# The output projection's weights in small pieces beside the token groups, their sums made by VectorE

## The reference

```python
x = x + 0.5 * ffn(layernorm(x), A, B, Wr)
x = x + attn(layernorm(x), wq, wkv, wo)
x = x + 0.5 * ffn(layernorm(x), A, B, Wr)
# in attn: attn is [tokens, 32 * 128], wo is [4096, 512]
attn = jnp.einsum('bhqk,bkhd->bqhd', probs, v).reshape(B, S, H * DV)
return jnp.einsum('bse,ed->bsd', attn, wo)
```

## Time and profile before

| | us |
|---|---|
| median of 3 runs | 1104.97 |
| lowest, highest | 1104.9, 1106.04 |
| the profiled execution | 1104.14 |
| its span, first to last instruction | 1102.3 |
| TensorE busy in the span | 1045.1 (95%) |
| VectorE, ScalarE, GpSimd busy | 697.0, 554.5, 563.5 |

### The profile page before, as it was taken

One profiled execution on the slowest core, in us unless ns is written; L12 is line 12 of the kernel. 1 busy time (PEld: TensorE's weight loads), 2 busy tenths in 40 slices (PEclk: granted clock), 3 DMA queues, 4 the chain that ended last, 5 costly groups with the idle time before them and its releaser, 6 DMA issues.

```text
span 1102.3 us, 18719 instructions
## 1 busy us (share of the span) xinstructions
PE 1045.1 (95%) x5588; PEld 899.3 (82%) x5588; DVE 697.0 (63%) x1803; ACT 554.5 (50%) x1480; POOL 563.5 (51%) x484
## 2 busy tenths in 40 slices
PE   8999999999999999999999999999677997799998
PEld 7999788888788888888888888888555876579997
DVE  6778734243476767676767776767569765565552
ACT  4112454544466666767666667676462544341110
POOL 5332288993667778877777788773055000000000
PEclk9999999999999999999999999999987998899999
DMA  9600255755334444444444444443942576540000
GB/s 370 274 0 1 109 197 219 258 210 186 102 115 134 151 154 139 147 135 150 126 135 148 152 139 147 143 158 108 393 170 95 174 272 249 228 137 10 19 19 29
DMA packets 77942, 168.16 MB, mean 153 GB/s; under 512 B 7888, under 2 KB 24272, under 8 KB 75856
## 3 DMA queue, kind: packets, MB, share of 16 engines
q1 hardware_dynamic: 77904, 167.67, 43.3%
HBM read 102.37 MB, written 63.44 MB: 150 GB/s over the span
## 4 chain that ended last, share of the span: by engine, by line
PE 85%; DMA 6%; DVE 5%; ACT 1%; POOL 1%; SPq 1%; issue 1%; DVEq 0%; ACTq 0%; POOLq 0%
PE bank L270 25%; PE bank L272 25%; PE bank L271 24%; DMA o_raw<-keep_o 5%; PE bank L530 4%; PE bank L548 2%; PE bank L519 2%; DVE o_lo L921 2%; PE bank L326 1%; DMA x<-x_in 1%; ACT o_hi L596 1%; POOL downT_lo L1614 1%; DVE ow_lo L921 1%; DVE wo_raw L1189 1%; PE bank L278 1%
## 5 line engine op out<-in xcount | busy, mean ns | idle before, releaser
L1242 POOL TENSOR_SCALAR ve<-mv 128x1 f32<-128x1 f32 x24 | 5.5, 230 | 294.1 <-DVE mv L928 293.8
L270 PE MATMUL bank<-o_lo,ow_hi 128*128 128x512 f32 x224 | 94.4, 421 | 39.4 <-DVE o_lo L921 35.8
L921 DVE TENSOR_TENSOR o_lo<-o_raw,o_hi 128x1024 fp32r<-128x1024 f32 x56 | 77.8, 1390 | 70.4 <-ACT o_hi L596 70.2
L596 ACT CAST o_hi<-o_raw 128x1024 fp32r<-128x1024 f32 x56 | 58.8, 1053 | 110.2 <-DMA o_raw<-keep_o 96.5
L642 ACT ACTIVATE bank<-bank,nmax 128x128 f32<-128x128 f32 (+1 forms) x256 | 105.7, 455 | 3.1 <-DVE nmax L1042 3.0
L1055 DVE TENSOR_SCALAR prob<-bank,rinv 128x128 f32<-128x128 f32 (+1 forms) x256 | 95.1, 413 | 4.6
L270 PE MATMUL bank<-xc_lo,wq_hi 128*128 128x512 f32 x224 | 93.6, 418 | 2.3 <-DVE qT_lo L921 1.2
L1042 DVE CUSTOM_DVE_ANT_0 bank<-bank,mask 128x128 f32<-128x128 f32 (+1 forms) x256 | 83.7, 389 | 19.1 <-PE bank L272 19.1
L272 PE MATMUL bank<-o_hi,ow_hi 128*128 128x512 f32 x224 | 92.0, 411 | 0.0
L271 PE MATMUL bank<-o_hi,ow_lo 128*128 128x512 f32 x224 | 92.0, 411 | 0.0
L270 PE MATMUL bank<-xc_lo,wk_hi 128*128 128x512 f32 x224 | 87.7, 391 | 1.8 <-DVE s7k L1083 1.5
(11 more groups left out here) (163 smaller groups left out, 3187.9 us busy)
## 6 DMA issues: line engine op xcount, KB each, us to landing
o_raw<-keep_o SPq DMA_DIRECT2D x49, 512.0 KB, 3.6
keep_v<-out_hl SPq DMA_DIRECT2D x64, 256.0 KB, 2.3
v<-keep_v SPq DMA_DIRECT2D x64, 256.0 KB, 3.6
keep_o<-att_comb SPq DMA_DIRECT2D x60, 256.0 KB, 2.5
keep_o<-att SPq DMA_DIRECT2D x45, 256.0 KB, 3.0
stage_v<-wv SPq DMA_DIRECT2D x4, 2048.0 KB, 9.2
stage_wq<-wqk SPq DMA_DIRECT2D x16, 512.0 KB, 3.3
keep_vraw<-out_raw SPq DMA_DIRECT2D x64, 128.0 KB, 2.1
```

The lines of the kernel that those rows point to most:

```text
L270: nc.tensor.matmul(dst, a_hi, b_lo, start=first, stop=False, skip_group_check=onto)
L596: return nc.scalar.copy(dst, src)
L921: return nc.vector.tensor_tensor(dst, src, hi.bitcast(F32), ALU.subtract)
```

## The change

- SyncE: the four transfers of 2 MB become 16 pieces of 512 KB, one behind the load of each group 1 to 16 (the table `WO_LOADS`; a11's two first blocks are now loaded a second time, into `wo_raw`, since s3 needs them). They share four semaphores, so that a piece waits for the landing of the fourth piece before it. The reloads become 16 pieces of the up weights (272 KB) behind groups 20 to 27 and 32 to 39, and 16 of the down weights (256 KB) behind groups 40 to 55.
- GpSimd makes no sums of weights any more.
- VectorE makes s3 ahead of groups 13, 15, 17, 20, s2 ahead of 14, 16, 18, 21 (as a22 - s3), s1 ahead of 25, 27, 29, 31 and s4 ahead of 33, 35, 37, 39. s3 now has the buffer that s1 had, and s1 lies in the place of a21.
- TensorE's six sets of transposes, VectorE's additions and the first layer norm of the next layer stand one group later where they moved.

```diff
+WO_LOADS = {1: ("a11", 2), 2: ("a11", 3), 3: ("a11", 0), 4: ("a11", 1), 5: ("a12", 0), 6: ("a12", 1), 7: ("a21", 0),
+            8: ("a22", 0), 9: ("a12", 2), 10: ("a21", 1), 11: ("a22", 1), 12: ("a12", 3), 13: ("a21", 2),
+            14: ("a22", 2), 15: ("a21", 3), 16: ("a22", 3)}
...
+        def wait_piece(eng, name, h):
+            n = PIECES.index((name, h))
+            eng.wait_ge(s[f"wo_piece{n % 4}"], 16 * (n // 4 + 1))
...
+        def dve_o_s3(dve, h):
+            for a in ("a11", "a21"):
+                wait_piece(dve, a, h)
+            if h == 0:
+                dve.wait_ge(s["scores_ready"], 8 * PAIRS)
+            nc.vector.tensor_tensor(wo_rows("s3", h), wo_rows("a11", h), wo_rows("a21", h), ALU.subtract).then_inc(s["wo_s3_s"], 1)
 
         def dve_o_s2(dve, h):
             dve.wait_ge(s["wo_s3_s"], h + 1)
-            nc.vector.tensor_tensor(wo_rows(S2, h), wo_rows(S1, h), wo_rows(A11, h), ALU.subtract).then_inc(s["wo_s2_s"], 1)
+            wait_piece(dve, "a22", h)
+            nc.vector.tensor_tensor(wo_rows("s2", h), wo_rows("a22", h), wo_rows("s3", h), ALU.subtract).then_inc(s["wo_s2_s"], 1)
...
         def dve_output(dve):
             for m in range(7, OGROUPS):
-                if m in (9, 11, 13, 15):
-                    dve_o_s2(dve, (m - 9) // 2)
+                if m in (13, 15, 17, 20):
+                    dve_o_s3(dve, (13, 15, 17, 20).index(m))
+                elif m in (14, 16, 18, 21):
+                    dve_o_s2(dve, (14, 16, 18, 21).index(m))
                 elif m in (25, 27, 29, 31):
-                    dve_o_s4(dve, (m - 25) // 2)
+                    dve_o_s1(dve, (m - 25) // 2)
+                elif m in (33, 35, 37, 39):
+                    dve_o_s4(dve, (m - 33) // 2)
                 elif m in (19, 43, 51):
                     dve_o_sum(dve, {19: 0, 43: 1, 51: 2}[m])
-                elif m in (22, 24, 46, 48):
-                    dve_back(dve, {22: 0, 24: 1, 46: 2, 48: 3}[m])
-                elif m == 52:
+                elif m in (23, 24, 47, 48):
+                    dve_back(dve, {23: 0, 24: 1, 47: 2, 48: 3}[m])
+                elif m == 53:
                     dve_back(dve, 4)
...
-        def pool_wo_sums(pool):
...
-            for h in range(4):
-                nc.gpsimd.tensor_tensor(wo_rows(S1, h), wo_rows(A21, h), wo_rows(A22, h), ALU.add).then_inc(s["wo_s1_s"], 1)
-                pool.wait_ge(s["wo_s1_s"], h + 1)
-                nc.gpsimd.tensor_tensor(wo_rows(S3, h), wo_rows(A11, h), wo_rows(A21, h), ALU.subtract).then_inc(s["wo_s3_s"], 1)
...
+        def load_wo(sp_, name, h):
+            n = ("a11", "a21", "a12", "a22").index(name)
+            i = PIECES.index((name, h))
+            if i >= 4:
+                sp_.wait_ge(s[f"wo_piece{i % 4}"], 16 * (i // 4))
+            sp_.dma_start(wo_raw[:, n, 4 * h:4 * h + 4, :].rearrange("p c n -> p (c n)"),
+                          wo[n][:, h * 8 * P:(h + 1) * 8 * P]).then_inc(s[f"wo_piece{i % 4}"], 16)
...
+        def load_beside(sp_, m):
+            if m in WO_LOADS:
+                load_wo(sp_, *WO_LOADS[m])
+            if 20 <= m < 28:
+                k, a = divmod(m - 20, 2)
+                load_again(sp_, upT_lo[:, k, :], keep_up[1][:, k * UPW:(k + 1) * UPW], "upagain_loaded", a)
+            elif 32 <= m < 40:
+                if m == 32:
+                    sp_.wait_ge(s["wo_split"], 16)
+                k, a = divmod(m - 32, 2)
+                load_again(sp_, upT_hi[:, k, :], keep_up[0][:, k * UPW:(k + 1) * UPW], "upagain_loaded", a)
+            elif m >= 40:
+                if m == 40:
+                    sp_.wait_ge(s["wo_s4_s"], 4)
+                    sp_.wait_ge(s["wo_split"], 20)
+                i, k = divmod(m - 40, 8)
+                load_again(sp_, (downT2_hi, downT2_lo)[i][:, k, :], keep_down[i][:, k * D:(k + 1) * D], "downagain_loaded")
...
-            load_tokens(sync, 1)
-            load_wo(sync, 0, "wo_a11")
-            load_tokens(sync, 2)
-            load_tokens(sync, 3)
+            for m in range(1, 4):
+                load_tokens(sync, m)
+                load_beside(sync, m)
             load_pair(sync, LAST, final=True)
-            load_wo(sync, 1, "wo_a21")
-            load_wo(sync, 3, "wo_a22")
-            for m in range(4, 7):
+            for m in range(4, OGROUPS):
                 load_tokens(sync, m)
-            load_wo(sync, 2, "wo_a12")
-            for m in range(7, OGROUPS):
-                load_tokens(sync, m)
-                if m == 4 * OG:
-                    sync.wait_ge(s["wo_split"], 16)
-                    sync.wait_ge(s["wo_s4_s"], 4)
-                    for i, t in enumerate((downT2_hi, downT2_lo)):
-                        sync.dma_start(t[:, :, :].rearrange("p k n -> p (k n)").bitcast(F32), keep_down[i]).then_inc(s["downagain_loaded"], 16)
-                elif m == 5 * OG:
-                    sync.wait_ge(s["wo_split"], 20)
-                    for i, t in enumerate((upT_hi, upT_lo)):
-                        sync.dma_start(t[:, :, :].rearrange("p k n -> p (k n)").bitcast(F32), keep_up[i]).then_inc(s["upagain_loaded"], 16)
+                load_beside(sync, m)
...
-            pool_wo_sums(pool)
...
-                if m in (18, 20, 42, 44, 49, 51):
-                    pe_back(pe, {18: 0, 20: 1, 42: 2, 44: 3, 49: 4, 51: 5}[m])
-                elif m == 54:
+                if m in (19, 21, 43, 45, 50, 52):
+                    pe_back(pe, {19: 0, 21: 1, 43: 2, 45: 3, 50: 4, 52: 5}[m])
+                elif m == 55:
                     pe_ffn_transpose(pe, NT)
```

More of the change, by code:

```diff
@@ L58 @@
 SLOTS = 3
-O_WEIGHT = (A11, A12, S2, S3, S1, A22, S4)
 O_TOKEN = (B11, B21, T2, T3, T1, N4, B22)
@@ L68 @@
 LAST = PAIRS - 1
+WO_LOADS = {1: ("a11", 2), 2: ("a11", 3), 3: ("a11", 0), 4: ("a11", 1), 5: ("a12", 0), 6: ("a12", 1), 7: ("a21", 0),
+            8: ("a22", 0), 9: ("a12", 2), 10: ("a21", 1), 11: ("a22", 1), 12: ("a12", 3), 13: ("a21", 2),
+            14: ("a22", 2), 15: ("a21", 3), 16: ("a22", 3)}
+PIECES = tuple(WO_LOADS.values())
 EPS = 1e-5
@@ L187, in build_macaron @@
         wo_raw = place("wo_raw", [P, 4, PAIRS, 2 * P], F32, at=where["xc_hi"])
-        wo_s1 = place("wo_s1", [P, PAIRS, 2 * P], F32, at=where["upT_hi"])
-        WO = {A11: wo_raw[:, 0, :, :], A21: wo_raw[:, 1, :, :], A12: wo_raw[:, 2, :, :], A22: wo_raw[:, 3, :, :],
-              S1: wo_s1[:, :, :], S2: wo_raw[:, 0, :, :], S4: wo_raw[:, 2, :, :]}
+        wo_s3 = place("wo_s3", [P, PAIRS, 2 * P], F32, at=where["upT_hi"])
+        WO = {"a11": wo_raw[:, 0, :, :], "a21": wo_raw[:, 1, :, :], "a12": wo_raw[:, 2, :, :], "a22": wo_raw[:, 3, :, :],
+              "s1": wo_raw[:, 1, :, :], "s2": wo_raw[:, 0, :, :], "s3": wo_s3[:, :, :], "s4": wo_raw[:, 2, :, :]}
+        O_OPERAND = ("a11", "a12", "s2", "s3", "s1", "a22", "s4")
         slot = 2 * 2 * P * 16
@@ L863, in o_weight_src, with wo_rows @@
             if k < 2:
-                return ow_raw[k][:, :, :]
-            return (WO[O_WEIGHT[i]] if O_WEIGHT[i] != S3 else wo_raw[:, 1, :, :])[:, 4 * h:4 * h + 4, :]
+                return ow_raw[k][:, :, :].rearrange("p c n -> p (c n)")
+            return wo_rows(O_OPERAND[i], h)
+        def wait_piece(eng, name, h):
+            n = PIECES.index((name, h))
+            eng.wait_ge(s[f"wo_piece{n % 4}"], 16 * (n // 4 + 1))
+        def wo_rows(op, h):
+            return WO[op][:, 4 * h:4 * h + 4, :].rearrange("p c n -> p (c n)")
         def act_o_weight(act, k):
@@ L1181, in dve_o_tokens, with dve_o_s1 @@
                o_hi[n][:, :, :].rearrange("p c n -> p (c n)")).then_inc(s["o_split"], 1)
-        def wo_rows(op, h):
-            t = wo_raw[:, 1, :, :] if op in (A21, S3) else WO[op]
-            return t[:, 4 * h:4 * h + 4, :].rearrange("p c n -> p (c n)")
+        def dve_o_s3(dve, h):
[4 more added lines that the diff above has]
+            nc.vector.tensor_tensor(wo_rows("s3", h), wo_rows("a11", h), wo_rows("a21", h), ALU.subtract).then_inc(s["wo_s3_s"], 1)
         def dve_o_s2(dve, h):
             dve.wait_ge(s["wo_s3_s"], h + 1)
-            nc.vector.tensor_tensor(wo_rows(S2, h), wo_rows(S1, h), wo_rows(A11, h), ALU.subtract).then_inc(s["wo_s2_s"], 1)
+            wait_piece(dve, "a22", h)
+            nc.vector.tensor_tensor(wo_rows("s2", h), wo_rows("a22", h), wo_rows("s3", h), ALU.subtract).then_inc(s["wo_s2_s"], 1)
+        def dve_o_s1(dve, h):
+            nc.vector.tensor_tensor(wo_rows("s1", h), wo_rows("a21", h), wo_rows("a22", h), ALU.add).then_inc(s["wo_s1_s"], 1)
         def dve_o_s4(dve, h):
             dve.wait_ge(s["wo_s2_s"], h + 1)
-            nc.vector.tensor_tensor(wo_rows(S4, h), wo_rows(A12, h), wo_rows(S2, h), ALU.subtract).then_inc(s["wo_s4_s"], 1)
+            nc.vector.tensor_tensor(wo_rows("s4", h), wo_rows("a12", h), wo_rows("s2", h), ALU.subtract).then_inc(s["wo_s4_s"], 1)
         def dve_o_sum(dve, block):
@@ L1452, in load_wo_first, with load_again @@
```

(9 more changed lines are left out.)

34 lines of the change are left out of this document (11 added, 23 removed).

## The result

The changed kernel takes 1061.34 us (median of 4 runs, 1060.21 to 1061.63) where the one before takes 1104.93 beside it (1104.35 to 1106.04): a ratio of 0.960, 95% interval 0.959 to 0.962. That is 43.6 us less; the forecast was 47.0 less, 1058.0, and its range 1053 to 1066. The time lies just above the narrower 1055 to 1061 that had the chance of 0.60. The profiled execution took 1061.25 us, its span 1059.5 against 1102.3.

A forecast was written before the change was run, and what follows sets the result against it. TensorE was taken as the engine to beat, held up in the output projection by late token loads and VectorE slowed beside GpSimd. Terms summed to 47.0 us: span 1102.3 to 1055.3, plus 2.7 gives 1058.0; range 1053 to 1066.

The forecast's parts named there:

- Part 1: Last head pair: output weights in 512 KB pieces remove the 8.18 stall and half clock; 11.3 us gained, bounds 8.0 to 12.
- Part 2: Groups 7 to 10: GpSimd's eight sums go to VectorE; 15.6 us gained, plus 1.7 from half clock after 843.96.
- the wait at group 21: TensorE's transposes ahead of group 21 wait 2.4 us for VectorE's addition, 1.8 longer than before; bounds 0.6 and 4.
- Part 3: FFN weight reloads in pieces: stalls of 8.28 and 7.24 and the half clock after them go; 19.5 us gained.
- Part 4: Moved transposes: the 1.7 us wait for csum goes; the second addition's 0.75 stays.
- Part 5: DMA in groups 7 to 16: a group with one piece needs 2.8 to 3.2 us; cost 1.0, bounds 0 and 3.
- What would show it: Signs in the next trace: token loads, TensorE waits, clock 1.00, VectorE near 1.2, group 7 near 806, FFN near 948.
- A: Rival: DMA bounds groups 7 to 17 at 3.2 to 3.5 us each; 5 to 10 us less gain; chance 0.12.
- B: Rival: full VectorE in groups 13 to 22, or the last pair, holds; 3.5 to 7 us less gain; chance 0.12.
- C: Rival: transfers of one group don't overlap, 4.5 us more in each of 42 groups, 1247 us; chance 0.04.
- D: Rival: pieces pile up behind SyncE's waits and come in a burst, one stall of 8; 1068 to 1075; chance 0.03.
- E: Better case: no wait at group 21 and none of DMA's, 3 to 4 us more gain, 1054 to 1055; chance 0.08.

The follow-up runs named there:

- the experiment: Changed kernel with a11, a21, a22 and a12 again loaded as whole 2 MB transfers at the old places; 1068.41 us.
- the two controls: The changed kernel run again unaltered, in the first and third batches of follow-up runs; 1062.81 us and 1061.87 us.
- the control: The changed kernel run again unaltered, in the first batch (also called the first control); 1062.81 us, ratio 0.962.
- the paired pieces: Changed kernel with the reloads' 32 pieces in pairs behind groups 20 to 23, 32 to 35 and 40 to 47; 1061.95 us.
- the later transposes: Changed kernel with the second and fourth transposes ahead of groups 22 and 46, last addition ahead of 49; 1056.79 us.
- the earlier sums and the earlier cast: Changed kernel with later transposes, s3 and s2 up to two groups earlier, group 7 cast before the last attention copy; 1054.47 us.

## Why the prediction was right, point by point

**Part 1, 11.3.** The stretch gained 9.3 in the traces, 9.2 in the experiment. The stall of 8.18 and its low clock went, though group 4's load, issued at 780.96, took until 789.1 to land and not until 785: TensorE comes to its group later still, at 795.17. Two things took back 2.2. The first group's 12 matmuls took 2.85 us before and 4.33 after (776.39 to 780.72), since the clock fell behind the same wait of 3.68; this is no part of the change (below). And a wait of 0.72 ahead of group 6 is new. VectorE's o_lo for it takes twice its time while GpSimd adds up the attention's output beside it. VectorE's timeline, then GpSimd's:

```profile
801.05 2.31 DVE L925 TENSOR_TENSOR o_lo<-o_raw,o_hi 128x1024 fp32r<-128x1024 f32 x1
```
```profile
799.91 2.37 POOL L1274 TENSOR_TENSOR att_comb<-att_comb,att 128x512 f32<-128x512 f32 x1
```

Before, the stall of group 4 and the half clock behind it had held TensorE up: that o_lo ended at 809.7, ahead of TensorE, which came to group 6 at 811.6. The sentence on "the next late one" named the softmax chain instead.

**Part 2, 15.6 + 1.7, and the wait at group 21.** From group 7 on VectorE's subtractions take 1.22 each and never more than 1.46, where one took 3.36; groups 7 to 10 take 11.0 us instead of 26.5. GpSimd's sums alone, even spread over the pieces' arrivals, cost 10.8. The full stretch from group 13 to 22 and its bill ahead of group 21 came as described: 1.93 where 2.4 was forecast, and one instruction behind another on VectorE when it comes to the addition for which TensorE waits:

```profile
847.87 1.23 DVE L925 TENSOR_TENSOR ow_lo<-wo_raw,ow_hi 128x1024 fp32r<-128x1024 f32 x1
849.01 1.22 DVE L925 TENSOR_TENSOR o_lo<-o_raw,o_hi 128x1024 fp32r<-128x1024 f32 x1
850.15 0.68 DVE L1222 TENSOR_TENSOR x<-bank,x 128x512 f32<-128x512 f32 x1
```

**Part 3, 19.5.** Measured alone: 19.75.

**Part 4, 1.7 gained, 0.75 to stay.** The wait for csum is gone. The second addition's wait did not stay at 0.75 but grew to 1.68: this term was too small by 0.9 (in the two controls the wait was 1.63 and 1.22). The reload's pieces run beside that stretch, and I gave them no price there ("Later groups ... fit"); that they are the cause, no run shows.

**Part 5, 1.0 for DMA.** A group with its piece needs 2.9 us by the trace, inside the 2.8 to 3.2. Taking the pieces away makes group 7 to the FFN 1.5 shorter than in the changed kernel's trace, and 3.5 shorter than in the control's, which had a fall of the clock behind group 21's wait besides. That is 1.5 for the pieces, where 1.0 was taken, and the rest is the clock's.

**The sum.** For group 7 to the FFN the terms give 15.6 + 1.7 + 19.5 + 1.7 - 1.8 - 1.0 = 35.7; measured 36.0. That is not luck. The first matmul of each group can be counted off on TensorE's timelines (12 to a group), and the parts come out one by one:

| groups | before | after | gained | forecast |
|---|---|---|---|---|
| 7 to 10 | 26.52 | 11.01 | 15.5 | 15.6 |
| 11 and 12 | 7.20 | 5.44 | 1.8 | 1.7 |
| 13 to 22 | 28.95 | 31.03 | -2.1 | -1.8 - 1.0 |
| 23 to the FFN | 114.87 | 94.07 | 20.8 | 19.5 + 1.7 |

In the first control groups 13 to 22 took 33.07, 2.0 more, mostly since the clock fell there (last section).

The 4.2 by which the span fell short (42.8 for 47.0) are 2.0 in the last pair, 1.25 ahead of it and 1.29 at the very end, less the 0.3 gained here. The 1.25 come from a wait near 26 us behind which the clock fell (0.79 granted in 24 to 32 us, 1.00 before). The 1.29 are the landing of the last store: 5.04 us from the last matmul to the end, 3.75 before. In the other kernels here, which issue the same instructions at this place, it was anywhere from 3.8 to 5.1 (twice 3.8, mostly 4.6 to 5.1), so one trace of each kernel can't show whether the change has a part in it. The time fell short by less, 1061.34 against 1058.0, and that is luck: the forecast added 2.7 to the span, from a median and a profiled execution that did not belong together, where 1.8 was right for both kernels (1104.14 - 1102.3, 1061.34 - 1059.5).

**What would show it.** No wait over 3 behind 780 and one wait of 1 to 3 us at the second transposes: right. VectorE near 1.2: right from group 7 on, wrong for group 6's 2.31. No token load over 6 us: right from 800 on, wrong ahead of it, where the last stores and the values share the queue. The token loads that went out in 780 to 800 and in 800 to 940:

```profile
DMA to landing us min/median/max: 2.4/4.6/8.1
```
```profile
DMA to landing us min/median/max: 2.7/3.8/5.1
```

Group 7 at 809.4 instead of 806 and the FFN at 950.9 instead of 948: 1.25 of each is the head's. "Clock 1.00 in all of it" was wrong, in this trace by the first group alone.

**The rivals.** A asked for lateness of 5 to 10 in groups 7 to 17: the pieces cost 1.5. B's "full VectorE" is real, but the waits at the second and fourth transposes are together 2.3 longer than before (1.93 + 1.68 for 0.57 + 0.75), of which the sum had 1.8, so it took 0.5 off the forecast and not 3.5 to 7. C is refuted by the paired pieces, D by those landings, 5.1 at most from 800 on where a burst would give a stall of 8. E, no wait at group 21 and none of DMA's, is what the later transposes reach: 1056.8, and 1054.5 with the earlier sums and the earlier cast.

**What stays open.** The three parts undone one by one cost 19.75, 10.8 and 5.6, 36.1 together, where the control of that batch lies 40.0 below the kernel before. The traces say the same: from the first group's matmul to the FFN they cost 19.8, 13.8 and 4.9 against the control's, 38.4 of the 42.5 between it and the kernel before. Undone together they would cost more, I take it, since pieces spread GpSimd's sums out (it waits 9.13 us for one). How the 4 us between divide wasn't measured.

## What to carry to other kernels

Where one in-order queue carries paced loads and bulk, cut the bulk until it holds up the load behind it for no longer than about the lead that the buffers give (here, with a lead of some 2 us and groups of 2.72, 1 MB cost nothing, 4 MB cost 7 to 9 us and some matmuls at the low clock behind it). Give sums with two inputs to GpSimd only where VectorE has idle time to lose in their company; where VectorE is full, each of its subtractions beside one took 3.3 to 3.4 us instead of 1.2. Once the large stalls are gone, look at each step that waits for another engine's answer, and put it one group later: here that was worth its two waits, 3.9 us for 3.6, and 2 us more against an execution in which the clock had fallen behind one of them.
